# A gated layer on one core: product blocks summed by a strided reduction, the G projection moved, routing as a sign

## The chip, the cores and the metric

The kernel runs on one core of a Trainium2 chip. The metric is the device time of one execution in microseconds; lower is better. The engines named below are TensorE (PE, with its weight loads as PEld), VectorE (DVE), ScalarE (ACT), GpSimd (POOL) and SyncE (SP), each with its own in-order queue.

## The reference

Input x is 16 x 256 x 512 (16 blocks, 256 rows, 512 time steps), and a context of the same shape. The layer has two parts:

```
# part 1: per head of 8 rows, 32 heads
kv  = outer product of the context's rows            # i, j, head, l
y   = causal convolution of kv with ssm_kernel[head] + kv * D[head]
x   = x + tanh(g_xattn) * sum_i y[i, j] * q[i]       # q = layernorm(x)
# part 2: on each row of 512, 16 blocks of a sequence
z   = layernorm(x)
y   = silu(z_prev * w0 + z * w1)
q, k, v, g = silu(y Wq), y Wk, y Wv, y Wg            # then rotary on q and k
route = argmax over 2 of (v . router_w)              # one of two slots per head and position
q_exp, k_exp = q or k placed in the slot of its route, zero in the other; q scaled by score / count
o   = (q_exp k_exp^T masked causally) v              # then normalized per head
x   = x + tanh(g_ffn) * (silu(g) * o) Wout
```

A product of q_exp and k_exp is the plain product where both positions have the same route, and zero where they differ.

## The kernel before

The kernel works through 32 heads of part 1 (8 rows of 16 blocks: one 128 x 512 tile), and `step(h)` is a software pipeline written out in Python for h = -2 to 32. Each engine has its own order of work within a step, written by hand, with semaphores between them. A step h does the following for different tiles: `pre` prepares head h+2 (context products on POOL, normalized q), `front` does the convolution of head h+1, `back` the projections, routing and scores of tile h, `tail` the attention output and the output projection of the tile before.

TensorE's order in a step is: transposes of z (L361), convolution chunks 0 and 1 (L290), attention output (L337), convolution chunk 2, transposes of oT (L377), the last half block (L303, L306), q and k projections with the logits (L319), convolution chunk 3, the rank matmul (L402), transposes of qn, the V projection into bank 4 (L411), transposes of `gated` (L418), the transposes of the sums (L422, by `add_transposed`, L277), the G projection into bank 5 (L426), transposes of `qke` (L428, L431), the output projection (L440) and the scores (L352).

The convolution's result is multiplied with q on DVE (`multiply`, L743 and L747, and `multiply_last`), which leaves eight product blocks of 128 columns per chunk of 128 time steps in `z_terms`, four chunks in all. DVE adds the upper four blocks to the lower four (`add_halves`, L756: chunks 0 and 1 in one instruction, chunks 2 and 3 in one each). TensorE then sums the remaining four in PSUM while it transposes them: sixteen accumulating 128 x 128 transposes into bank 2, after which `xo_ps` is signalled. DVE reads bank 2 in L889 (x2), takes statistics (L892 to L900), POOL takes the root (L649), ACT makes the scaled mean and z (L610, L614), and z is transposed at the head of the next step.

Routing: the logit difference sits in bank 6. DVE writes `sel`, two 0/1 masks for q and k (L840, L841), and `u`, which is +0.5 or -0.5 (L842), used by the rank matmul that counts positions of a route. POOL applies the rotary factors to q and k (L667; L672 twice, one half of the columns each; L675, the sum into `rot_a`), and DVE expands the result into `qke` (L765, 1024 columns: two slots, each masked).

Three waits matter around the change. The V projection writes bank 4 and waits for `o_normed`, which DVE's L856 signals when it has read the attention output of the tile before from that bank. The transposes of `qke` wait for `qke_ready` (L765); those of k also for `gatedT_ready` (L877), which frees bank 7. The scores wait for `x2_ready`.

DVE's order after the half block is: L840 to L842, the add of chunks 0 and 1, L856, L861 (`gated`), the reciprocal L864, products of chunk 3, the adds of chunks 2 and 3, L873, L877, L765, L889 and the statistics, L903, L913 (output), then the four score masks (L760).

Of the kernel before, what the change touches and what calls it, by code (L numbers as in the profile page):

```python
# [13 lines left out]
P = 128  # L14
# [15 lines left out]
def flamingo_gated_layer(nc, x, ctx_t, g_xattn, g_ffn, ssm_kernel, ssm_D, conv_w, Wq, Wk, Wv, Wg,  # L30
# [35 lines left out]
    with ExitStack() as stack:  # L66
# [50 lines left out]
        u = sb("u", RH)  # L117
        sel = sb("sel", 2, RH, RATIO)
# [10 lines left out]
        setup = ExitStack()  # L129
        w_all = setup_sb("w_all", CH, PROJ)  # L130
# [4 lines left out]
        taps = setup_sb("taps", P + L)  # L135
        taps_p = setup.enter_context(nc.sbuf_tensor("taps_p", [P, 2, P + L], F32R))
        setup.close()

        y_raw = sb("y_raw", CH, P)
        qk_sb = sb("qk_sb", 2 * RH, HDK)  # L140
# [4 lines left out]
        qke = sb("qke", 2 * RH, RATIO * HDK)  # L145
# [7 lines left out]
        yT_p = parts("yT", CH, P)  # L153
# [111 lines left out]
        def _(eng):  # L265
# [5 lines left out]
            def add_transposed(h1):  # L271


                for c in range(CH):
                    eng.wait_ge(sum_done[max(c, 1)], h1 + 1)
                    for i in range(NROT):
                        ins = nc.tensor.matmul(bank[2][:, c * P:(c + 1) * P], z_terms[:, c, i * ROW:(i + 1) * ROW], ident,  # L277
                                               is_transpose=True, start=(c == 0 and i == 0), stop=(i == NROT - 1),
                                               skip_group_check=True)
                ins.then_inc(xo_ps, 1)  # L280
# [45 lines left out]
            def step(t, p, q, tail, back, front, pre):  # L326
# [72 lines left out]
                if back:  # L399
                    eng.wait_ge(u_ready, h + 1)  # L400
                    eng.wait_ge(qk_copied, h + 1)
                    nc.tensor.matmul(bank[6][:, 0:RH], rank, u[:, :], start=True, stop=True).then_inc(cnt_ps, 1)  # L402
# [16 lines left out]
                if front:  # L419
                    if pre:  # L420
                        eng.wait_ge(qx_ready, h + 3)
                    add_transposed(h + 1)  # L422
                if back:
                    if can_wait(h):
                        eng.wait_ge(mask_done[2], h)
                    project(bank[5], yT_p, w_all_p, G0, DV, g_ps, y_low, h + 1)  # L426
                    eng.wait_ge(qke_ready, h + 1)
                    transpose4(bank[3], lambda c: qke[:, 4 * c:4 * c + 4, :], qeT_ps)  # L428
                    if tail:
                        eng.wait_ge(gatedT_ready, h)  # L430
                    transpose4(bank[7], lambda c: qke[:, RH + 4 * c:RH + 4 * c + 4, :], keT_ps)  # L431
# [15 lines left out]
        def _(eng):  # L447
# [41 lines left out]
            def step(t, p, q, tail, back, front, pre):  # L489
# [60 lines left out]
                if back:  # L550
                    eng.wait_ge(q_ps, h + 1)
                    if can_wait(h):
                        eng.wait_ge(rot_prod, 3 * h)
                    eng.activation(qk_sb[:, 0:RH, :], bank[3][:, 0:DK].rearrange("p (a n) -> p a n", n=HDK),
                                   ACT.Silu)
                    eng.wait_ge(logit_ps, h + 1)
                    eng.activation(qk_sb[:, RH:2 * RH, :], bank[6][:, 0:DK].rearrange("p (a n) -> p a n", n=HDK),  # L557
                                   ACT.Copy).then_inc(qk_copied, 1)
                    if can_wait(h):
                        eng.wait_ge(rth1_ready, h)  # L560
                    eng.activation(ad[:, :], bank[6][:, DK:DK + RH], ACT.Abs).then_inc(ad_ready, 1)
                    eng.wait_ge(ad_ready, h + 1)
                    eng.activation(th[:, :], ad[:, :], ACT.Tanh, scale=0.5).then_inc(th_ready, 1)
                    eng.wait_ge(th_ready, h + 1)
                    eng.activation(th1[:, :], th[:, :], ACT.Copy, bias=1.0).then_inc(th1_ready, 1)
# [24 lines left out]
                if pre:  # L590
                    kv_round(p, 2, h + 2)
                    kv_round(p, 3, h + 2)
                if back:
# [3 lines left out]
                    eng.activation(gate_sb[:, :], bank[5][:, :], ACT.Silu).then_inc(gate_ready, 1)  # L597
                if back:
                    eng.wait_ge(qeT_ps, h + 1)
                    if can_wait(h):  # L600
                        for r in range(CH):
# [5 lines left out]
                                   ).then_inc(keT_sb, 1)  # L607
                if front:
# [11 lines left out]
        def _(eng):  # L620
# [30 lines left out]
            def step(t, p, q, tail, back, front, pre):  # L651
# [10 lines left out]
                if back:  # L662

                    eng.wait_ge(qk_copied, h + 1)
                    if can_wait(h):
                        eng.wait_ge(qke_ready, h)
# [3 lines left out]
                    for a in range(2):  # L670
                        s = const[:, C_SIN + a * hf:C_SIN + a * hf + 1]
                        eng.tensor_tensor(rot_b[:, :, a * hf:(a + 1) * hf], qk_sb[:, :, (1 - a) * hf:(2 - a) * hf],  # L672
                                          view(s, [[0, 2 * RH], [1, hf]]), ALU.mult).then_inc(rot_prod, 1)
                    eng.wait_ge(rot_prod, 3 * h + 3)
                    eng.tensor_tensor(rot_a[:, :, :], rot_a[:, :, :], rot_b[:, :, :], ALU.add).then_inc(rot_ready, 1)  # L675
# [12 lines left out]
        def _(eng):  # L688
# [3 lines left out]
            eng.memset(u[:, :], 0.0).then_inc(taps_ready, 1)  # L692
# [40 lines left out]
            def multiply(p, lc, h1):  # L733
# [3 lines left out]
                if lc == 0:  # L737
                    eng.wait_ge(qx_ready, h1 + 1)
                    if can_wait(h1):
                        eng.wait_ge(xo_ps, h1)  # L740
# [10 lines left out]
            def add_halves(chunks, h1):  # L751

                eng.wait_ge(mul_last, h1 + 1)
                eng.wait_ge(mul_done[chunks.stop - 1], h1 + 1)
                half = NROT * ROW
                eng.tensor_tensor(z_terms[:, chunks, 0:half], z_terms[:, chunks, 0:half], z_terms[:, chunks, half:2 * half],  # L756
                                  ALU.add).then_inc(sum_done[chunks.stop - 1], 1)
# [5 lines left out]
            def expand():  # L763

                eng.tensor_tensor(view(qke[:, 0, 0:1], [[RATIO * HDK, 2 * RH], [HDK, RATIO], [1, HDK]]),  # L765
                                  view(rot_a[:, 0, 0:1], [[HDK, 2 * RH], [0, RATIO], [1, HDK]]),
                                  view(sel[:, 0, 0, 0:1], [[RATIO, 2 * RH], [1, RATIO], [0, HDK]]),
                                  ALU.mult).then_inc(qke_ready, 1)
# [16 lines left out]
            def step(t, p, q, tail, back, front, pre):  # L785
# [47 lines left out]
                if back:  # L833
# [5 lines left out]
                    d = view(bank[6][:, DK:DK + 1], [[0, 2], [1, RH]])  # L839
                    eng.tensor_scalar(sel[:, :, :, 0], d, 0.0, None, ALU.is_le)  # L840
                    eng.tensor_scalar(sel[:, :, :, 1], d, 0.0, None, ALU.is_gt)  # L841
                    eng.tensor_scalar(u[:, :], bank[6][:, DK:DK + RH], 0.0, 0.5, ALU.is_gt, ALU.subtract).then_inc(u_ready, 1)  # L842
# [7 lines left out]
                if front:  # L850
                    add_halves(slice(0, 2), h + 1)
# [13 lines left out]
                if front:  # L865
                    multiply(p, 3, h + 1)
                    add_halves(slice(2, 3), h + 1)
                    add_halves(slice(3, 4), h + 1)
# [10 lines left out]
                if back:  # L879
                    eng.wait_ge(rot_ready, h + 1)  # L880
                    if can_wait(h):
                        eng.wait_ge(keT_ps, h)
                        eng.wait_ge(qeT_ps, h)
                    expand()
# [40 lines left out]
def shape_constants(NB, HDK):  # L925
# [8 lines left out]
    parts = [np.eye(P), same * HDK ** -0.5, rank, cos, cos, -sin, sin]  # L934
# [35 lines left out]
```

## Time and profile before

| | us |
|---|---|
| median of 3 runs | 923.17 (922.25 to 925.02) |
| profiled execution | 923.74 |
| its span | 921.9 |
| PE busy | 856.9 (93%) |
| DVE busy | 720.5 (78%) |
| ACT busy | 435.7 (47%) |
| POOL busy | 730.2 (79%) |

The span is the time from the first to the last record of the execution; what lies around it (1.8 us) is launch and end. Busy shares are averages over the whole span. Matmuls are pipelined, and the durations of neighbouring ones overlap: what one costs is read from the chain of waits, where each item begins when the one before it ends. In the order of time, "idle before" stands in brackets with the instruction that ended it.

### The profile page before, as it was taken

To read this page: it belongs to the slowest core of one execution; us is meant where nothing else is said; L and a number is where in the kernel's file an instruction comes from. 1 tells how busy PE (TensorE), PEld (TensorE's weight loads), DVE (VectorE), ACT (ScalarE), POOL (GpSimd) and SP (SyncE) were. 2 spreads that over 40 slices of the span, in tenths; PEclk is the share of its full clock that TensorE was granted. 3 is DMA by queue.
4 is the path that set the end of the run, shared out by engine and by line. 5 is a ranking of instruction groups with operands and counts; after the bars stand their busy time and mean duration, and the time that the engine had idled before them with its cause. 6 is when DMAs were issued, how large, how long until landed. Compare 5 with 4: busy or idle time off the path is not lost.

```text
span 921.9 us, 17871 instructions
## 1 busy us (share of the span) xinstructions
PE 856.9 (93%) x6528; PEld 724.3 (79%) x6528; DVE 720.5 (78%) x1528; ACT 435.7 (47%) x938; POOL 730.2 (79%) x613
## 2 busy tenths in 40 slices
PE   0578999999999999999999999999999999999973
PEld 0467888888888888888888888888888888888852
DVE  4867787987778889877787897778878877788742
ACT  2454544545545444554544545545445455454330
POOL 6568898788889888888899888888988888887331
PEclk9889999999999999999999999999999999999996
DMA  8211211222221122222211222222112222210000
GB/s 284 60 53 52 59 26 44 64 63 65 64 64 43 25 61 64 64 64 65 62 34 35 61 64 64 65 63 61 26 42 64 64 64 63 64 46 12 2 12 23
DMA packets 25990, 52.44 MB, mean 57 GB/s; under 512 B 2544, under 2 KB 3696, under 8 KB 25904
## 3 DMA queue, kind: packets, MB, share of 16 engines
q1 hardware_dynamic: 22304, 46.59, 18.7%
q10 hardware_dynamic: 3600, 4.72, 1.6%
q8 instruction: 52, 0.85, 0.4%
q14 instruction: 34, 0.28, 0.1%
HBM read 42.75 MB, written 8.55 MB: 56 GB/s over the span
## 4 chain that ended last, share of the span: by engine, by line
PE 86%; DVE 5%; issue 4%; DMA 1%; ACT 1%; POOL 1%; POOLq 0%; ACTq 0%; DVEq 0%
PE bank L319 37%; PE bank L290 23%; PE bank L268 9%; PE bank L277 6%; PE bank L352 4%; PE bank L337 4%; PE bank L303 2%; DMA w_all<-in_L_ffn_Wv 1%; PE bank L306 1%; DVE z_terms L756 1%; DVE w_all L719 0%; PE bank L402 0%; DVE z_terms L743 0%; DVE w_all_low L725 0%; POOLq L66 0%
## 5 line engine op out<-in xcount | busy, mean ns | idle before, releaser
L290 PE MATMUL bank<-kv_pair,toep 128*128 128x512 f32 x960 | 247.9, 405 | 11.4 <-DVE z_terms L747 6.6
L643 POOL TENSOR_TENSOR kv_pair<-kv,kv_pair 128x576 fp32r<-128x576 f32 x128 | 182.3, 1436 | 54.9 <-ACT kv_pair L487 54.9
L290 PEld LDWEIGHTS bank<-kv_pair,toep 128*128 128x128 f32 x960 | 177.2, 192 | 53.1 <-DVE z_terms L747 12.6
L634 POOL TENSOR_TENSOR kv<-kx 128x512 f32<-128x512 f32 x128 | 174.4, 1363 | 6.7 <-DMA const<-shape_consts 6.7
L649 POOL TENSOR_TENSOR o_rstd<-o_ve,minus_half 128x16 f32<-128x16 f32 x32 | 93.1, 2909 | 82.6 <-DVE o_ve L815 82.6
L487 ACT ACTIVATE kv_pair<-kv 128x576 fp32r<-128x576 f32 x128 | 87.9, 688 | 108.2 <-POOL kv L637 108.2
L319 PE MATMUL bank<-w_all_high,yT_high 128*128 128x512 f32 (+2 forms) x512 | 120.2, 356 | 2.8 <-DVE gated L856 2.8
L756 DVE TENSOR_TENSOR z_terms<-z_terms 128x512 f32<-128x512 f32 (+1 forms) x96 | 117.4, 1249 | 0.0
L319 PE MATMUL bank<-w_all_low,yT_high 128*128 128x512 f32 (+2 forms) x512 | 111.8, 340 | 0.0
L319 PE MATMUL bank<-w_all_high,yT_low 128*128 128x512 f32 (+2 forms) x512 | 106.1, 339 | 0.0
L913 DVE TENSOR_TENSOR out_sb<-bank,x 128x512 f32<-128x512 f32 x32 | 22.1, 691 | 105.6 <-PE bank L319 105.6
L760 DVE TENSOR_TENSOR att<-bank,const 128x512 f32<-128x512 f32 x128 | 79.5, 683 | 16.7 <-PE bank L352 16.7
L319 PEld LDWEIGHTS bank<-w_all_low,yT_high 128*128 128x128 f32 x512 | 83.7, 189 | 11.2
L319 PEld LDWEIGHTS bank<-w_all_high,yT_low 128*128 128x128 f32 x512 | 81.2, 188 | 11.5
L743 DVE TENSOR_TENSOR z_terms<-bank,qx 128x512 f32<-128x512 f32 x128 | 85.4, 667 | 4.3 <-PE bank L290 4.3
L319 PEld LDWEIGHTS bank<-w_all_high,yT_high 128*128 128x128 f32 x512 | 78.9, 190 | 8.9 <-DVE gated L856 3.2
L637 POOL TENSOR_TENSOR kv<-kx 128x64 f32<-128x64 f32 x128 | 73.5, 574 | 0.0
L747 DVE TENSOR_TENSOR z_terms<-bank,qx 128x384 f32<-128x384 f32 x128 | 69.9, 546 | 0.0
L667 POOL TENSOR_TENSOR rot_a<-qk_sb,const 128x512 f32<-128x512 f32 x32 | 66.2, 2069 | 2.5 <-ACT qk_sb L557 2.5
L277 PE MATMUL bank<-const,z_terms 128*128 128x128 f32 x512 | 62.5, 274 | 5.4 <-DVE z_terms L756 5.4
L503 ACT ACTIVATE y_raw<-bank,w_conv 128x128 f32<-128x128 f32 x128 | 36.6, 369 | 61.9 <-PE bank L268 61.9
L649 POOL TENSOR_TENSOR rstd<-ve,minus_half 128x1 f32<-128x1 f32 x64 | 41.2, 643 | 28.3 <-DVE ve L900 22.2
(102 smaller groups left out, 1588.7 us busy)
## 6 DMA issues: line engine op xcount, KB each, us to landing
toep<-taps_dram SPq DMA_DIRECT2D x32, 512.0 KB, 7.1
kx<-in_ctx SPq DMA_DIRECT2D x32, 384.0 KB, 7.4
x_in<-in_x SPq DMA_DIRECT2D x32, 256.0 KB
out_x<-out_sb SPq DMA_DIRECT2D x32, 256.0 KB
w_all<-in_L_ffn_Wv ACTq DMA_DIRECT2D x1, 1024.0 KB, 11.9
w_all<-in_L_ffn_Wg ACTq DMA_DIRECT2D x1, 1024.0 KB, 9.9
w_out<-in_L_ffn_Wout ACTq DMA_DIRECT2D x1, 1024.0 KB, 16.2
router<-in_L_ffn_router_w ACTq DMA_DIRECT2D x1, 512.0 KB, 7.3
```

The source lines that it names most:

```text
L268: ins = nc.tensor.transpose(dst[:, c * P:(c + 1) * P], src(c), ident)
L277: ins = nc.tensor.matmul(bank[2][:, c * P:(c + 1) * P], z_terms[:, c, i * ROW:(i + 1) * ROW], ident, is_transpose=True, start=(c == 0 and ...
L290: ins = nc.tensor.matmul(bank[lc % 2][:, :], toep[:, 1 - p, a, (lc - mc) * P:(lc - mc + 1) * P], kv_p[b][:, 1 - p, mc, 0:FULL], start=(mc ...
L319: ins = nc.tensor.matmul(dst[:, 0:cols], src_p[a][:, c, :], w_p[b][:, c, c0:c0 + cols], start=(i == 0 and c == 0), stop=(i == len(PASSES) ...
L487: eng.activation(kv_p[0][:, p, c, :], kv[:, c % 2, :], ACT.Copy).then_inc(kv_high[c], 1)
L634: eng.tensor_tensor(view(kv[:, c % 2, 0:FULL], [[ROW, NROT], [1, ROW]]), view(kx[:, p, c, 0:ROW], [[0, NROT], [1, ROW]]), view(kx[:, p, c, ...
L637: eng.tensor_tensor(kv[:, c % 2, FULL:FULL + HALF], kx[:, p, c, 0:HALF], kx[:, p, c, HALF:2 * HALF], ALU.mult).then_inc(kv_made[c], 1)
L643: eng.tensor_tensor(kv_p[1][:, p, c, :], kv[:, c % 2, :], kv_p[0][:, p, c, :].bitcast(F32), ALU.subtract).then_inc(kv_ready[c], 1)
L649: eng.tensor_tensor(dst[:, 0:n], src[:, 0:n], minus_half[:, 0:n], ALU.pow).then_inc(done, 1)
L743: eng.tensor_tensor(view(z_terms[:, lc, 0:1], [[ROW, NROT], [1, ROW]]), view(y[:, 0:1], [[ROW, NROT], [1, ROW]]), view(q, [[NB, NROT], [1, ...
L756: eng.tensor_tensor(z_terms[:, chunks, 0:half], z_terms[:, chunks, 0:half], z_terms[:, chunks, half:2 * half], ALU.add).then_inc(sum_done[ ...
L760: eng.tensor_tensor(att[:, r, :, :], bank[SCORE_BANKS[r]][:, :].rearrange("p (c n) -> p c n", c=CH), view(mask[:, 0:1], [[0, CH], [1, P]]) ...
```

## The change

Three things change together. First, the eight product blocks of a chunk are summed by one `tensor_reduce` on DVE that reads with a stride of 128 columns between the eight numbers of a sum and writes 128 sums to `z_sum` (the memory of `y_raw`); TensorE transposes the four chunks once each. Second, the order changes: on TensorE the G projection comes before the sums' transposes; on ACT the gate follows `gatedT` directly, and the two late `kv_round` calls are spread; on DVE the last step of `qke` comes before L873 and L877. Third, routing: `qke` holds q or k in its even columns (written by POOL's rotary sum) and the same times a sign of +1 or -1 in its odd columns (written by DVE); the causal factor is halved in the constants, so that equal signs give the product and different ones zero. `sel` is gone, `u` has a copy for k, and the two half-width products of POOL are one instruction. Memory is laid out anew so that `y_raw` and `yT` don't lie over weights still in use at the start.

```diff
-        sel = sb("sel", 2, RH, RATIO)
+        u = sb("u", 2, RH)
+        z_sum = y_raw
-        qke = sb("qke", 2 * RH, RATIO * HDK)
+        qke = sb("qke", 2 * RH, HDK, RATIO)
...
-            def add_transposed(h1):
+            def transpose_sums(h1):
                 for c in range(CH):
-                    eng.wait_ge(sum_done[max(c, 1)], h1 + 1)
-                    for i in range(NROT):
-                        ins = nc.tensor.matmul(bank[2][:, c * P:(c + 1) * P], z_terms[:, c, i * ROW:(i + 1) * ROW], ident,
-                                               is_transpose=True, start=(c == 0 and i == 0), stop=(i == NROT - 1),
-                                               skip_group_check=True)
+                    eng.wait_ge(sum_done[c], h1 + 1)
+                    ins = nc.tensor.transpose(bank[2][:, c * P:(c + 1) * P], z_sum[:, c, :], ident)
                 ins.then_inc(xo_ps, 1)
...
+                if back:
+                    if can_wait(h):
+                        eng.wait_ge(mask_done[2], h)
+                    project(bank[5], yT_p, w_all_p, G0, DV, g_ps, y_low, h + 1)
                 if front:
                     if pre:
                         eng.wait_ge(qx_ready, h + 3)
-                    add_transposed(h + 1)
-                if back:
-                    if can_wait(h):
-                        eng.wait_ge(mask_done[2], h)
-                    project(bank[5], yT_p, w_all_p, G0, DV, g_ps, y_low, h + 1)
+                    transpose_sums(h + 1)
...
-                if pre:
-                    kv_round(p, 2, h + 2)
-                    kv_round(p, 3, h + 2)
                 if back:
                     ... gate_sb (Silu) ...
+                if pre:
+                    kv_round(p, 2, h + 2)
                 if back:
                     ... qeT, keT ...
+                if pre:
+                    kv_round(p, 3, h + 2)
...
-                    for a in range(2):
-                        s = const[:, C_SIN + a * hf:C_SIN + a * hf + 1]
-                        eng.tensor_tensor(rot_b[:, :, a * hf:(a + 1) * hf], qk_sb[:, :, (1 - a) * hf:(2 - a) * hf],
-                                          view(s, [[0, 2 * RH], [1, hf]]), ALU.mult).then_inc(rot_prod, 1)
-                    eng.wait_ge(rot_prod, 3 * h + 3)
-                    eng.tensor_tensor(rot_a[:, :, :], rot_a[:, :, :], rot_b[:, :, :], ALU.add).then_inc(rot_ready, 1)
+                    sin = const[:, C_SIN:C_SIN + 1]
+                    eng.tensor_tensor(view(rot_b[:, 0, 0:1], [[HDK, 2 * RH], [hf, 2], [1, hf]]),
+                                      view(qk_sb[:, 0, hf:hf + 1], [[HDK, 2 * RH], [-hf, 2], [1, hf]]),
+                                      view(sin, [[0, 2 * RH], [hf, 2], [1, hf]]), ALU.mult).then_inc(rot_prod, 1)
+                    eng.wait_ge(rot_prod, 2 * h + 2)
+                    if can_wait(h):
+                        eng.wait_ge(keT_ps, h)
+                        eng.wait_ge(qeT_ps, h)
+                    eng.tensor_tensor(qke[:, :, :, 0], rot_a[:, :, :], rot_b[:, :, :], ALU.add).then_inc(rot_ready, 1)
...
-            def add_halves(chunks, h1):
-                eng.wait_ge(mul_last, h1 + 1)
-                eng.wait_ge(mul_done[chunks.stop - 1], h1 + 1)
-                half = NROT * ROW
-                eng.tensor_tensor(z_terms[:, chunks, 0:half], z_terms[:, chunks, 0:half], z_terms[:, chunks, half:2 * half],
-                                  ALU.add).then_inc(sum_done[chunks.stop - 1], 1)
+            def sum_terms(c, h1):
+                eng.wait_ge(mul_last, h1 + 1)
+                eng.wait_ge(mul_done[c], h1 + 1)
+                if can_wait(h1):
+                    eng.wait_ge(xo_ps, h1)
+                eng.tensor_reduce(z_sum[:, c, :], view(z_terms[:, c, 0:1], [[1, ROW], [ROW, 2 * NROT]]), AX_X, ALU.add
+                                  ).then_inc(sum_done[c], 1)
...
-            def expand():
-                eng.tensor_tensor(view(qke[:, 0, 0:1], [[RATIO * HDK, 2 * RH], [HDK, RATIO], [1, HDK]]),
-                                  view(rot_a[:, 0, 0:1], [[HDK, 2 * RH], [0, RATIO], [1, HDK]]),
-                                  view(sel[:, 0, 0, 0:1], [[RATIO, 2 * RH], [1, RATIO], [0, HDK]]),
-                                  ALU.mult).then_inc(qke_ready, 1)
+            def signed_copy():
+                eng.scalar_tensor_tensor(out=qke[:, :, :, 1], in0=qke[:, :, :, 0], scalar=2.0,
+                                         in1=view(u[:, 0, 0:1], [[1, 2 * RH], [0, HDK]]), op0=ALU.mult, op1=ALU.mult
+                                         ).then_inc(qke_ready, 1)
...
-                    d = view(bank[6][:, DK:DK + 1], [[0, 2], [1, RH]])
-                    eng.tensor_scalar(sel[:, :, :, 0], d, 0.0, None, ALU.is_le)
-                    eng.tensor_scalar(sel[:, :, :, 1], d, 0.0, None, ALU.is_gt)
-                    eng.tensor_scalar(u[:, :], bank[6][:, DK:DK + RH], 0.0, 0.5, ALU.is_gt, ALU.subtract).then_inc(u_ready, 1)
+                    eng.tensor_scalar(u[:, :, :], view(bank[6][:, DK:DK + 1], [[0, 2], [1, RH]]), 0.0, 0.5, ALU.is_gt, ALU.subtract).then_inc(u_ready, 1)
...
-                    add_halves(slice(0, 2), h + 1)
+                    sum_terms(0, h + 1)
+                    sum_terms(1, h + 1)
...
-                    add_halves(slice(2, 3), h + 1)
-                    add_halves(slice(3, 4), h + 1)
+                    sum_terms(2, h + 1)
+                    sum_terms(3, h + 1)
+                if back:
+                    eng.wait_ge(rot_ready, h + 1)
+                    if can_wait(h):
+                        eng.wait_ge(keT_ps, h)
+                        eng.wait_ge(qeT_ps, h)
+                    signed_copy()
...
-    parts = [np.eye(P), same * HDK ** -0.5, rank, cos, cos, -sin, sin]
+    parts = [np.eye(P), same * HDK ** -0.5 / 2, rank, cos, cos, -sin, sin]
```

In the new order `multiply` of chunk 0 waits for the last sum and no longer for `xo_ps`.

## Rows read from the trace of the kernel before

**Rows 1.** Stretches, busy us (x count) of PE, PEld, DVE, ACT, POOL, then clock

```profile
356.00:412.00 56.00, 55.82 (x428) 47.50 (x427) 46.44 (x103) 28.29 (x65) 48.45 (x41) 1.00 0.20 53
```

**Rows 2.** Chain of waits, one step: start us, us, what

```profile
413.43 2.78 PE bank L319 x12
416.21 0.44 PE bank L268 x4
416.65 1.75 PE bank L277 x16
418.40 2.78 PE bank L319 x12
...
422.05 2.75 PE bank L319 x12
424.80 1.10 PE bank L352 x32
...
439.86 2.78 PE bank L319 x12
```

**Rows 3.** Chain of waits, transposes of z of steps 1 and 30

```profile
81.05 0.59 PE bank L268 x4
...
849.21 0.59 PE bank L268 x4
```

**Rows 4.** Order of time, one step on DVE: start us, us, engine, line, operation

```profile
406.70 0.69 DVE L812 TENSOR_REDUCE o_var<-o_sq 128x16 f32<-128x512 f32 x1
...
410.77 0.18 DVE L840 TENSOR_SCALAR sel<-bank 128x32 f32<-128x32 f32 x1
...
411.05 1.22 DVE L756 TENSOR_TENSOR z_terms<-z_terms 128x1024 f32<-128x1024 f32 x1
...
412.18 0.69 DVE L856 TENSOR_TENSOR gated<-bank,o_rstd 128x512 f32<-128x512 f32 x1
...
413.16 0.76 PEld L319 LDWEIGHTS bank<-w_all_high,yT_high 128*128 128x128 f32 x4
...
415.06 2.43 DVE L756 TENSOR_TENSOR z_terms<-z_terms 128x512 f32<-128x512 f32 x2
...
418.09 1.56 DVE L765 TENSOR_TENSOR qke<-rot_a,sel 128x1024 f32<-128x1024 f32 x1
```

**Rows 5.** Order of time at the start, DVE and POOL

```profile
14.67 1.70 DVE L702 TENSOR_TENSOR router_d<-router 128x512 f32<-128x512 f32 x1 [0.66 <-DMA w_all<-in_L_ffn_Wv]
...
15.78 0.77 POOL L637 TENSOR_TENSOR kv<-kx 128x64 f32<-128x64 f32 x1
...
44.05 1.28 DVE L756 TENSOR_TENSOR z_terms<-z_terms 128x512 f32<-128x512 f32 x2
```

**Rows 6.** Order of time, then the chain, last step with a convolution

```profile
860.60 2.06 DVE L756 TENSOR_TENSOR z_terms<-z_terms 128x1024 f32<-128x1024 f32 x1
...
863.31 0.76 PEld L319 LDWEIGHTS bank<-w_all_high,yT_high 128*128 128x128 f32 x4 [0.73 <-DVE gated L856]
...
863.31 3.06 PE bank L319 x12
```

**Rows 7.** Order of time, POOL at step 0 and in the step of rows 4

```profile
64.11 1.27 POOL L667 TENSOR_TENSOR rot_a<-qk_sb,const 128x512 f32<-128x512 f32 x1 [2.53 <-ACT qk_sb L557]
...
411.23 2.18 POOL L667 TENSOR_TENSOR rot_a<-qk_sb,const 128x512 f32<-128x512 f32 x1
```

**Rows 8.** Order of time, from the sums to z in the same step

```profile
419.58 0.74 DVE L889 SCALAR_TENSOR_TENSOR x<-bank,gates,x_in 128x512 f32<-128x512 f32 x1
...
421.37 0.14 DVE L900 TENSOR_SCALAR ve<-mv 128x1 f32<-128x1 f32 x1
...
423.76 0.81 ACT L614 ACTIVATE z<-x,nmr,rstd 128x512 f32<-128x512 f32 x1
```

**Rows 9.** Order of time, TensorE at step 0

```profile
73.36 0.71 PEld L277 LDWEIGHTS bank<-const,z_terms 128*128 128x128 f32 x4 [1.20 <-DVE z_terms L756]
...
74.13 2.06 PE L319 MATMUL bank<-w_all_high,yT_high 128*128 128x512 f32 x4
```

More of the change, by code:

```diff
@@ L116, in flamingo_gated_layer @@
         ad = sb("ad", RH)
-        u = sb("u", RH)
-        sel = sb("sel", 2, RH, RATIO)
+        u = sb("u", 2, RH)
         th = sb("th", RH)
@@ L129, in flamingo_gated_layer @@
         setup = ExitStack()
+        taps = setup_sb("taps", P + L)
+        taps_p = setup.enter_context(nc.sbuf_tensor("taps_p", [P, 2, P + L], F32R))
         w_all = setup_sb("w_all", CH, PROJ)
@@ L134, in flamingo_gated_layer @@
         router_d = setup_sb("router_d", RH * HDV)
-        taps = setup_sb("taps", P + L)
-        taps_p = setup.enter_context(nc.sbuf_tensor("taps_p", [P, 2, P + L], F32R))
         setup.close()
         y_raw = sb("y_raw", CH, P)
+        z_sum = y_raw
+        yT_p = parts("yT", CH, P)
         qk_sb = sb("qk_sb", 2 * RH, HDK)
@@ L152, in flamingo_gated_layer @@
         out_sb = sb("out_sb", 2, L)
-        yT_p = parts("yT", CH, P)
         gatedT_p = parts("gatedT", CH, P)
@@ L401, in step @@
                     eng.wait_ge(qk_copied, h + 1)
-                    nc.tensor.matmul(bank[6][:, 0:RH], rank, u[:, :], start=True, stop=True).then_inc(cnt_ps, 1)
+                    nc.tensor.matmul(bank[6][:, 0:RH], rank, u[:, 0, :], start=True, stop=True).then_inc(cnt_ps, 1)
                 if pre:
@@ L418, in step @@
                     transpose4(bank[7], lambda c: gated[:, c * P:(c + 1) * P], gatedT_ps)
-                if front:
-                    if pre:
-                        eng.wait_ge(qx_ready, h + 3)
-                    add_transposed(h + 1)
                 if back:
@@ L426, in step @@
                     project(bank[5], yT_p, w_all_p, G0, DV, g_ps, y_low, h + 1)
+                if front:
+                    if pre:
+                        eng.wait_ge(qx_ready, h + 3)
+                    transpose_sums(h + 1)
+                if back:
                     eng.wait_ge(qke_ready, h + 1)
-                    transpose4(bank[3], lambda c: qke[:, 4 * c:4 * c + 4, :], qeT_ps)
+                    transpose4(bank[3], lambda c: qke[:, 4 * c:4 * c + 4, :, :], qeT_ps)
                     if tail:
                         eng.wait_ge(gatedT_ready, h)
-                    transpose4(bank[7], lambda c: qke[:, RH + 4 * c:RH + 4 * c + 4, :], keT_ps)
+                    transpose4(bank[7], lambda c: qke[:, RH + 4 * c:RH + 4 * c + 4, :, :], keT_ps)
                 if tail:
@@ L552, in step @@
                     if can_wait(h):
-                        eng.wait_ge(rot_prod, 3 * h)
+                        eng.wait_ge(rot_prod, 2 * h)
                     eng.activation(qk_sb[:, 0:RH, :], bank[3][:, 0:DK].rearrange("p (a n) -> p a n", n=HDK),
@@ L589, in step @@
                                    ).then_inc(gatedT_high, 1)
-                if pre:
-                    kv_round(p, 2, h + 2)
-                    kv_round(p, 3, h + 2)
                 if back:
@@ L607, in step @@
                                    ).then_inc(keT_sb, 1)
+                if pre:
+                    kv_round(p, 3, h + 2)
                 if front:
@@ L665, in step @@
                     if can_wait(h):
-                        eng.wait_ge(qke_ready, h)
+                        eng.wait_ge(rot_ready, h)
                     eng.tensor_tensor(rot_a[:, :, :], qk_sb[:, :, :], view(const[:, C_COS:C_COS + 1], [[0, 2 * RH], [1, HDK]]),
@@ L691, in _ @@
             eng.tensor_tensor(taps[0:NH, P:P + 1], taps[0:NH, P:P + 1], d_tap[0:NH, :], ALU.add).then_inc(taps_zero, 1)
-            eng.memset(u[:, :], 0.0).then_inc(taps_ready, 1)
+            eng.memset(u[:, :, :], 0.0).then_inc(taps_ready, 1)
             eng.wait_ge(taps_high, 1)
@@ L739, in multiply @@
                     if can_wait(h1):
-                        eng.wait_ge(xo_ps, h1)
+                        eng.wait_ge(sum_done[CH - 1], h1)
                 q = qx[:, 1 - p, lc, 0:1]
```

4 lines of the change are left out of this document (removed).

## The prediction

> **What bounds the kernel now.** I read the stretches first, then the chain of waits, then the order of time on each engine. In 356 to 412 us TensorE is busy for 55.82 of 56.00 us at full granted clock, DVE for 46.44, POOL for 48.45 [rows 1]. TensorE is thus the bound in the middle, and the others have room only on average. The chain of waits is almost nothing but TensorE there, one item after the other without a gap [rows 2]. One step (one head) is 26.43 us, read between two starts of the V projection, 413.43 and 439.86; between two starts of the transposes of z, 81.05 and 849.21, lie 29 steps of 26.49 [rows 2, 3]. So what TensorE no longer issues is won, unless another engine hands something over too late. The whole question is how late DVE is at each hand-over.
>
> **TensorE's own work.** The sixteen accumulating transposes of the product blocks are one item of the chain, 1.75 us, 109 ns each. Four plain transposes of the same size are 0.44 us (those of `gated`) [rows 2]. The change leaves four: 1.75 - 0.44 = 1.31 us less per step. The G projection (2.78) moves ahead of them and costs the same there [rows 2]. With no new wait a step would be 26.46 - 1.31 = 25.15 us.
>
> **DVE before the V projection: the step that decides.** TensorE may write bank 4 only when DVE has read it in L856 (`o_normed`). Now L856 runs from 412.18 to 412.87, and the first weight load of the V projection starts at 413.16: 0.29 us of slack [rows 4]. In front of L856 stands the sum of chunks 0 and 1. It is one add of 1024 results now, 1.22 us, with the next instruction 1.13 after its start [rows 4]. The change puts two reductions there, each reading 1024 numbers. The trace has no such reduction, so its price is bounded. L812 reads 512 contiguous numbers in 0.69 us; 512 more at one per cycle, the rate between the add of 1024 (1.13) and the adds of 512 when nobody disturbs them (two in 1.28, row at 44.05), are 0.53 [rows 4, 5]. That gives 1.22 us for one, 1.13 from start to start. Below, it can't be under an undisturbed add of 512 results, which reads the same 1024 numbers through two inputs: 0.61 [rows 5]. Above, the slowest strided read in the trace is the subtraction L702, 512 results in 1.70 us, or 3.4 us for 1024 [rows 5]. I take 1.13, because L812 is the same operation and only its stride differs. Two of them are 2.26, that is +1.13. Of the three small instructions L840 to L842 (410.77 to 411.05, 0.28 us) one of 32 columns is left, started 0.10 before its successor: -0.18 [rows 4]. L856 therefore ends 0.95 us later, at 413.82, and the weight load can start at 413.87 and not at 413.16: 0.71 us late. DVE's clock up to here hangs on the end of the scores (masks, then convolution products, then statistics), which is TensorE's own work, so the delay doesn't average out; it returns in each step.
>
> The trace has this stall once. In the last step with a convolution the add took 2.06 us instead of 1.22, and the V projection's weight load stood idle for 0.73 until L856 was done, 863.31 [rows 6]. The chain then gives the projection 3.06 us instead of 2.78, since the overlap of loads with the matmuls before is lost too. From 413.87 it ends at 416.93 against 416.21 now: TensorE loses 0.72 of the 1.31. Net 0.59 per step, a step of 25.87.
>
> **Between POOL and DVE.** Instructions with two inputs in SBUF exclude each other on these two engines: POOL's L667 took 2.18 us while the add ran beside it, and 1.27 at step 0 where nothing did [rows 7]. The reductions have one input; I take it that they neither wait nor block. POOL's rotation gets earlier by this and by the merged `rot_b`; it was never late for DVE. I take POOL's strided write to `qke` at nothing: it is no longer waited for until 419.1; if it cost another 0.5 us, it would hold L861 for as long and use up slack only.
>
> **After the V projection.** All times from here are of the old clock, shifted as above. V ends at 416.93, the transposes of `gated` at 417.37, G at 420.15, the sums' transposes at 420.59, those of `qke` at 421.46. On DVE 2.19 us lie now between L856's end and the adds of chunks 2 and 3 (L861, reciprocal, products of chunk 3) [rows 4]. I add 0.8, since L861 meets POOL's third rotary instruction, 413.8 to 415.1 by three times 1.27 from 411.23 [rows 7]. So the reductions start at 416.8 and take 2.26 (the two disturbed adds 2.43 [rows 4]); the last sum is there at 419.1, needed at 420.15. The signed copy has 512 results and two inputs: 0.7 us against L765's 1.56 [rows 4]; it ends at 419.8 and is needed at 420.59. L877 follows and ends at 420.5, needed at 421.03. All is in time, by 0.5 to 1.0 us. What the cover costs if it is gone: each microsecond beyond that is one of the step.
>
> **The loop through z.** The transposes of the sums will end 4.7 us before those of the next z (0.87, 2.75, 1.10) and not 7.5 us [rows 2]. The chain behind them: L889 at 419.58 to L900 done at 421.51 is 1.93; from there to z done at 424.57 it is 3.06 now, with three copies ahead in ACT's queue; without them I put 1.9, of which z is 0.81 [rows 8]. With 3.85 us it fits by 0.9; with the whole 3.06 it would be 0.3 late. DVE must be free at 420.6, and is by 0.1. `kv_round(3)`, moved between `keT` and the mean on ACT, has its product by then and ends before the root does. POOL runs its last two `kv_rest` about 1.7 us later against TensorE; its idle time, 7.55 of 56 us or 3.6 per step [rows 1], takes that up.
>
> **Start and end.** At step -1, where DVE is the bound, four reductions (4.5) stand for adds of 1.2 and 1.28 [rows 4, 5], less 0.7 of transposes: +1.3. At step 0 TensorE waited 1.20 us for the last sum with the G projection behind it, which then ran at the lower clock, 2.06 us for four matmuls [rows 9]. Now it runs in that wait: the z transposes come at 78.3 and not 81.05 [rows 3], -2.7. The last step with a convolution has a stall already; there 1.31 - 0.1 = 1.2 is won. Behind it nothing.
>
> **Sum.** 29 x 0.59 = 17.1, and 1.2, and 2.7 - 1.3 = 1.4: 19.7 us off. The profiled execution took 923.74 (span 921.9), so 904.0; it lies 0.6 above the median of the runs. I forecast 904.
>
> **A rule that speaks against it.** The only strided read on DVE, L702 (every second float), took 1.70 us, but POOL held an instruction until 15.78, and from there it took 0.6, as an undisturbed one: no cost of stride to be seen [rows 5]. The Trainium skill (Advanced Engine Details and Errata, SBUF Cachelines) says that SBUF has lines of 16 bytes and that an access to a new line each time pays a penalty; a stride of 8 bytes has two hits on a line, the new reads, 512 bytes apart, none. It gives no figure; by that rule the reductions are slower and the sum above falls. No row here shows it.
>
> **Rivals.**
> - A, strided reads at half rate (chance 0.12). A reduction then takes 2.2 us from start to start. L856 ends 2.14 later still, V ends at 419.07; the last sum comes at 422.8 against G's end at 422.3, and the copy and L877 hold the last transposes by another 0.7. A step is then 29.0: 923.7 + 30 x 2.6 = 1001. It decides from 1.42 us per reduction (0.3 above mine) on: there the 0.59 is gone. Against it: L702; for it: nothing in the profile has such a stride.
> - B, DVE's second half is the bound (0.15). The signed copy or L861 meets one more POOL instruction (1.2 us) and L877 and L889 come 1.2 later. The transposes of k wait 0.7 and z is 0.2 late: a step of 26.5, and 921. For it: the adds of chunks 2 and 3 took 1.2 us each where 0.61 is undisturbed [rows 4, 5]. Against: POOL has done its products at 418.2 and waits for rsqrt by then.
> - C, no stall (0.08): something ahead of L856 gets shorter, such as the reduction at its lower bound. 31 x 1.31 = 41 off: 883.
> - The forecast (0.65): 895 to 914, from reductions 0.15 shorter to 0.15 longer (30 x 0.3 = 9 us each way).
>
> **Range and chances.** 890 to 925 takes in the forecast and B and leaves out A and C, 0.20. This kernel's measurement tells 0.3%, 2.8 us. Faster: 0.65 + 0.08 + 0.04 of B = 0.77; same: 0.07; slower: 0.12 + 0.04 = 0.16.
>
> **What would show it.** Right: a step of 25.9 us; on TensorE one idle item of 0.7 us per step ahead of the V projection, released by L856; the sums' transposes at 0.44; reductions of 1.22 us; L667 back at 1.3 us. Wrong: reductions well off 1.22; waits of TensorE for `qke`, for the low part of `gated` or for z; or no idle time ahead of V.

## The result and the profile after

The changed kernel takes 988.73 us (median of 4 runs, 987.17 to 994.32) against 923.63 beside it: 1.072 times as long, 95% interval 1.067 to 1.076. The forecast was 904, in 890 to 925. The profiled execution has a span of 985.4 us against 921.9.

Two of the costliest groups of the changed kernel's page. Each line gives line, engine, operation, out<-in, shapes and count, then busy us and mean ns of one, then the engine's idle time before them and what ended it.

```profile
L759 DVE TENSOR_REDUCE y_raw<-z_terms 128x128 f32<-128x1024 f32 x128 | 246.3, 1963 | 0.1
L316 PE MATMUL bank<-w_all_high,yT_high 128*128 128x512 f32 (+2 forms) x512 | 121.5, 359 | 61.2 <-DVE gated L856 61.2
```

A reduction takes 1.96 us and not the 1.22 of the forecast, and TensorE stands idle for 61 us in all until L856 is done. The next rows are one step in the order of time, on DVE, POOL and TensorE's weight loads (start us, us). They are the counterpart of [rows 4] and [rows 7]:

```profile
435.68 0.69 DVE L814 TENSOR_REDUCE o_var<-o_sq 128x16 f32<-128x512 f32 x1
...
439.75 0.18 DVE L841 TENSOR_SCALAR u<-bank 128x32 f32<-128x32 f32 x1
439.87 3.87 DVE L759 TENSOR_REDUCE y_raw<-z_terms 128x128 f32<-128x1024 f32 x2
440.21 1.30 POOL L666 TENSOR_TENSOR rot_a<-qk_sb,const 128x512 f32<-128x512 f32 x1
...
443.67 0.67 DVE L856 TENSOR_TENSOR gated<-bank,o_rstd 128x512 f32<-128x512 f32 x1
...
444.39 0.76 PEld L316 LDWEIGHTS bank<-w_all_high,yT_high 128*128 128x128 f32 x4 [2.25 <-DVE gated L856]
```

The two reductions occupy DVE for 3.80 us (439.87 to 443.67), 1.90 each from start to start. The rest is as forecast. `u` starts 0.12 us before its successor, POOL's first rotary product (L667 before, now L666) is back at 1.30 us, and the V projection's weight load starts as soon as L856 is done (444.34). Only the price of the reductions is another. Later in a step two small waits follow, for the copy into `qke` and for L883 (L877 before):

```profile
422.51 0.68 DVE L768 SCALAR_TENSOR_TENSOR qke<-qke,u 128x512 f32<-128x512 f32 x1
...
423.24 0.42 PEld L268 LDWEIGHTS bank<-const,qke 128*128 128x128 f32 x4 [0.46 <-DVE qke L768]
...
423.92 0.42 PEld L268 LDWEIGHTS bank<-const,qke 128*128 128x128 f32 x4 [0.26 <-DVE gatedT_low L883]
```

**Where 63.5 us of span went.** The scores (L349, L352 before) of step 0 start at 84.28 (79.87 before): 4.4 us. The 30 steps from there to the scores of step 30, at 938.70 (874.89 before), take 854.4 us and not 795.0: 59.4. The tail is 0.3 shorter. Of the 30 steps most take 28.2 us, but ten take about 28.95 and the first 29.76. Two neighbouring stretches of one step's length differ in the granted clock, which is the number behind the busy us of PE, PEld, DVE, ACT and POOL:

```profile
300.00:328.20 28.20, 26.36 (x190) 22.01 (x191) 24.41 (x47) 13.21 (x29) 19.10 (x19) 0.94 0.19 53
328.20:356.40 28.20, 25.80 (x194) 21.06 (x193) 25.11 (x48) 13.54 (x29) 19.79 (x19) 1.00 0.19 52
```

In the first of them, the matmuls behind TensorE's idle 2 us run slower for a while. The second and third group below took 1.10 and 1.09 us in the G projection of the same step, and the granted clock is 0.50 in the stretch from 303 to 305 us:

```profile
301.76 1.20 PE L316 MATMUL bank<-w_all_high,yT_high 128*128 128x512 f32 x4 [2.01 <-DVE gated L856]
302.79 1.71 PE L316 MATMUL bank<-w_all_low,yT_high 128*128 128x512 f32 x4
304.30 1.91 PE L316 MATMUL bank<-w_all_high,yT_low 128*128 128x512 f32 x4
```

```profile
303.00:305.00 2.00, 2.00 (x6) 1.60 (x5) 2.00 (x5) 0.00 (x0) 1.88 (x3) 0.50 0.00 0
```

So the clock went from 2.4 to 1.2 GHz for a part of this projection after the idle time. It does so in about every third step. The eleven long steps take 10 x 0.75 + 1.5 = 9 us of the 59.

### The profile page after: what moved, and what is told of

It reads as the page before. It is cut to its first block and busy times, and to the rows that moved or that the text cites. A ratio compares the mean times of both kernels' runs of the same rounds, so it can differ in the third digit from the quotient of the medians.

```text
span 985.4 us, 17102 instructions
## 1 busy us (share of the span) xinstructions
PE 851.8 (86%) x6144; PEld 697.1 (71%) x6144; DVE 827.6 (84%) x1496; ACT 443.5 (45%) x938; POOL 641.4 (65%) x581
## 5 line engine op out<-in xcount | busy, mean ns | idle before, releaser
L759 DVE TENSOR_REDUCE y_raw<-z_terms 128x128 f32<-128x1024 f32 x128 | 246.3, 1963 | 0.1
L633 POOL TENSOR_TENSOR kv<-kx 128x512 f32<-128x512 f32 x128 | 159.9, 1249 | 6.5 <-DMA const<-shape_consts 6.5
L316 PE MATMUL bank<-w_all_low,yT_high 128*128 128x512 f32 (+2 forms) x512 | 119.5, 358 | 0.0
L316 PE MATMUL bank<-w_all_high,yT_low 128*128 128x512 f32 (+2 forms) x512 | 113.2, 355 | 0.0
L316 PEld LDWEIGHTS bank<-w_all_low,yT_high 128*128 128x128 f32 x512 | 88.2, 198 | 12.5
L316 PEld LDWEIGHTS bank<-w_all_high,yT_low 128*128 128x128 f32 x512 | 86.8, 199 | 13.5
L581 ACT ACTIVATE v_sb<-bank 128x512 f32<-128x512 f32 x32 | 19.1, 598 | 149.6 <-PE bank L316 149.6
L636 POOL TENSOR_TENSOR kv<-kx 128x64 f32<-128x64 f32 x128 | 55.6, 435 | 0.0
L592 ACT ACTIVATE gate_sb<-bank 128x512 f32<-128x512 f32 x32 | 19.1, 598 | 68.7 <-PE bank L316 68.7
```

Source lines behind the costliest of these rows:

```text
L316: ins = nc.tensor.matmul(dst[:, 0:cols], src_p[a][:, c, :], w_p[b][:, c, c0:c0 + cols], start=(i == 0 and c == 0), stop=(i == len(PASSES) ...
L633: eng.tensor_tensor(view(kv[:, c % 2, 0:FULL], [[ROW, NROT], [1, ROW]]), view(kx[:, p, c, 0:ROW], [[0, NROT], [1, ROW]]), view(kx[:, p, c, ...
L636: eng.tensor_tensor(kv[:, c % 2, FULL:FULL + HALF], kx[:, p, c, 0:HALF], kx[:, p, c, HALF:2 * HALF], ALU.mult).then_inc(kv_made[c], 1)
L759: eng.tensor_reduce(z_sum[:, c, :], view(z_terms[:, c, 0:1], [[1, ROW], [ROW, 2 * NROT]]), AX_X, ALU.add).then_inc(sum_done[c], 1)
```

## The experiments

All times are medians beside runs of the kernel before on the same chip, and a ratio is the time over that of the kernel before, with its 95% interval. Diffs are cut short and are against the changed kernel, if nothing else is said. A step is read between two starts of the scores.

### Distance or number of results

```diff
-  view(z_terms[:, c, 0:1], [[1, ROW], [ROW, 2 * NROT]])      # 128 results of 8, 512 bytes apart
+  view(z_terms[:, c, 0:1], [[2 * NROT, ROW], [1, 2 * NROT]]) # e1_contiguous: neighbours
+  view(z_terms[:, c, 0:1], [[1, ROW], [ROW, NROT]])          # e2_four_blocks: half the numbers
```

> The changed kernel, but each reduction reads its 1024 numbers in the order of memory (8 neighbours per result) and not 512 bytes apart; the number of results, 128, stays, so the sums are of the wrong blocks and only the time is of use. The changed kernel has 1.96 us per reduction. Theory S (the distance between the numbers costs): 1.22 us per reduction, an idle 0.7 us ahead of the V projection, 895 to 914 us in all. Theory R (each result costs, 128 here against the 16 of L814): 1.96 us and 988 us, as changed.

> The changed kernel, but each reduction sums blocks 0 to 3 alone and leaves out 4 to 7: 512 numbers, the same distance, the same 128 results. Theory S: (1.96 - 0.15) / 1024 = 1.77 ns per number read, so 0.15 + 512 x 1.77 ns = 1.06 us per reduction, and 893 to 903 us. Theory R: 0.15 + 0.53 for the numbers + 128 x 5.8 ns for the results = 1.43 us, and 912 to 925 us.

e1_contiguous: 905.93 us, 0.980 of before (0.979 to 0.982). Below are the group of its reductions, from the groups by form, and the start of the V projection, from the order of time:

```profile
L759 DVE TENSOR_REDUCE y_raw<-z_terms 128x128 f32<-128x1024 f32 x128 | 149.7, 1210 | 0.1
```

```profile
405.15 0.68 DVE L856 TENSOR_TENSOR gated<-bank,o_rstd 128x512 f32<-128x512 f32 x1
...
405.89 0.76 PEld L316 LDWEIGHTS bank<-w_all_high,yT_high 128*128 128x128 f32 x4 [0.74 <-DVE gated L856]
```

A reduction takes 1.21 us, TensorE's weight loads are idle for 0.74 us ahead of V, and a step takes 25.89 (scores at 364.39 and 390.28). This is the forecast kernel, in its price, its wait (0.71), its step (25.87) and its time (904).

e2_four_blocks: 898.06 us, 1.074 us per reduction. Theory S said 0.15 + 512 x 1.77 ns = 1.06; the 1.43 of theory R is refuted. So the distance between the numbers costs, (1963 - 1210) / 1024 = 0.74 ns per number on top of about 1.04, and the number of results doesn't.

### From which distance on

```diff
+  view(z_terms[:, c, 0:1], [[6, ROW], [(2, 4, 8, 16)[c], 2 * NROT]])   # 8, 16, 32, 64 bytes
```

> The changed kernel with a different distance between the eight numbers of a result in each chunk's reduction: 8 bytes in chunk 0, 16 in chunk 1, 32 in chunk 2, 64 in chunk 3, 24 bytes from result to result; the sums are of the wrong numbers and only the durations are of use. If the price comes with every number that does not follow its neighbour, all four take 1.96 us. If it comes with a new 16-byte line per number, chunk 0 takes less (towards 1.2 to 1.6) and chunks 1 to 3 the same 1.96. If it grows with distance, the four rise one after the other.

The run took 948.65 us (one execution, for its durations alone). The rows are DVE's order of time: chunks 0 and 1 together, then chunks 1, 2 and 3, each by itself in a narrower stretch:

```profile
423.26 3.15 DVE L759 TENSOR_REDUCE y_raw<-z_terms 128x128 f32<-128x1024 f32 x2
```

```profile
424.39 2.01 DVE L759 TENSOR_REDUCE y_raw<-z_terms 128x128 f32<-128x1024 f32 x1
```

```profile
429.14 2.14 DVE L759 TENSOR_REDUCE y_raw<-z_terms 128x128 f32<-128x1024 f32 x1
```

```profile
431.18 1.97 DVE L759 TENSOR_REDUCE y_raw<-z_terms 128x128 f32<-128x1024 f32 x1
```

Chunk 0, 8 bytes apart, takes 424.39 - 423.26 = 1.13 us from start to start, as contiguous ones do. At 16, 32 and 64 bytes a reduction takes 2.01, 2.14 and 1.97 us, and 1.96 at 512 bytes. The jump lies between 8 and 16 bytes, and the price doesn't grow with the distance behind it.

The Trainium skill (Advanced Engine Details and Errata, SBUF Cachelines) says of lines of 16 bytes that it takes at least two hits on one to absorb the access. These four durations agree, and e1_contiguous has given the figure, 0.74 ns per number. L702, which reads every second float, had two hits.

### The rest of the change by itself

```diff
+  # e3_old_sums: add_halves and the sixteen accumulating transposes of before, in the new order
```

> The changed kernel with its new order and its routing by a sign, but with the sums of before: adds of halves on DVE and sixteen accumulating transposes. If the reductions alone made the change slow, TensorE is the bound again with a step of 26.4 us, and the start gains up to 3 us: 918 to 924. If the new order or the routing has a cost of its own, TensorE shows new waits for qke, z or gatedT and the time is over 928.

920.14 us, 0.995 (0.994 to 0.997). From 300 to 600 us TensorE waits for DVE only ahead of the convolution (L289, 0.2 us per step, as L290 did before), and the scores follow each other by 26.4 us (366.98, 393.40). The new order and the routing by a sign have no cost of their own and gain 4 us, nearly all at the start (the scores of step 0 begin at 75.48 instead of 79.87). The signed copy took 1.63 us there, against 0.68 in the changed kernel, while POOL had products of its own, and no wait for it shows.

```diff
+  # e11_sums_alone: the kernel before with the reductions and four plain transposes, old order, old routing
```

> The kernel before with the strided reductions and the four plain transposes alone: its old order and its old routing (and the new memory layout, which the sums need). The reductions are then late twice: V waits 2.4 us for L856, and the transposes of the sums, still ahead of the G projection, wait another 2.8 us with G behind them. A step of 30 us, 1020 to 1040. If only the wait ahead of V costs, 990.

1054.62 us, 1.141 (1.138 to 1.143): 66 us more than the changed kernel, and 15 more than the upper end of what I expected. Waits of TensorE in 300 to 600 us (total, times, longest):

```profile
PEld bank L277 <- DVE y_raw L754: 27.1, 20, 1.7
PEld bank L316 <- DVE gated L855: 23.6, 10, 2.4
```

Both waits of the expectation are there, 2.36 and 2.7 us per step. Steps are 30.2 us, and from the sixth on every third is 31.6 to 31.8. The expectation had left out the clock; these eight steps take about 11 us more than the others. The wait of 2.7 us is about as long as the G projection (2.78), which stands in that place in the changed kernel and has no such wait there. That G ahead of the sums is what spares the changed kernel this wait is argued from these two lengths; the routing differs as well, and no run moves G by itself.

### The reductions behind L856

```diff
-                    sum_terms(0, h + 1); sum_terms(1, h + 1)      # ahead of L856
+                    sum_terms(0, h + 1); sum_terms(1, h + 1)      # e4_sums_late: behind the reciprocal
```

> The changed kernel with the reductions of chunks 0 and 1 behind L856, L861 and the reciprocal on DVE. If the wait of the V projection is all that costs, it goes (2.2 us per step) and the time is about 915. If DVE is the bound for the rest of the step as well, which four reductions of 1.9 us make likely, the wait moves to the transposes of the sums and of qke: a step of 27.9 us, 970 to 978.

999.15 us, 1.081 (1.079 to 1.083), slower than the changed kernel. No wait ahead of the V projection is left. The largest waits of TensorE in 300 to 600 us (total, times, longest) are

```profile
PEld bank L276 <- DVE y_raw L759: 25.3, 22, 1.7
...
PEld bank L268 <- DVE qke L768: 4.6, 10, 0.5
```

The wait has only moved: four reductions make DVE the bound of the whole step. Its step is 28.15 us, near the expected 27.9. But every second or third lasts 29.7, such as the one from 372.58 to 402.31 at a granted clock of 0.94. The expectation of 970 to 978 had left that out: 14 steps longer by 1.6 make 22 us.

### The distance on the writing side

```diff
+  view(z_terms[:, lc, 0:1], [[1, NROT], [2 * NROT, ROW]])    # e8_interleaved: products written 32 bytes apart
+  view(z_terms[:, c, 0:1], [[2 * NROT, ROW], [1, 2 * NROT]]) # and read as neighbours
```

> The distance on the writing side: the products are written 32 bytes apart, eight blocks interleaved, and the reduction reads them contiguously in 1.21 us; the second product's rotation is left out, so that the numbers are not the reference's, but count and size of the instructions are. If DVE's writes pay nothing for distance: 905 us as with the contiguous reduction. If they pay as the reads did, 0.75 ns per number, L745 goes from 0.67 to 1.05 and L749 from 0.55 to 0.83, and 3 us more per step stand on DVE: over 950.

In this run the rotation of the second product is left out too, so that its sums are not the reference's; the count and the size of the instructions are. 1012.15 us, 1.093 (1.091 to 1.095). From the groups by form:

```profile
L745 DVE TENSOR_TENSOR z_terms<-bank,qx 128x512 f32<-128x512 f32 x128 | 145.0, 1133 | 4.1 <-PE bank L287 4.1
L749 DVE TENSOR_TENSOR z_terms<-bank,qx 128x384 f32<-128x384 f32 x128 | 115.8, 905 | 0.0
```

They were 667 and 546 ns in the changed kernel: (1133 - 667) / 512 = 0.91 ns per number written 32 bytes apart, a little more than a read pays. The reductions are back at 1.20 us, and still TensorE waits 2.3 us per step for L856, with the slower products ahead of it. Moving the distance to the other side gains nothing.

### Adds instead of reductions

```diff
+  # e5_tree_two: contiguous adds, 8 blocks to 4 (two instructions), 4 to 2 (one), eight transposes
+  # e6_tree_three: and 2 to 1 (one), four transposes
```

> The changed kernel, its order and its routing, but the sums on DVE are adds of contiguous halves, two levels deep: eight blocks to four (chunks 0 and 1 in one instruction ahead of L856, chunks 2 and 3 in one), then four to two (all chunks in one, 1024 results); TensorE sums the last two in eight accumulating transposes. If contiguous reads and little work ahead of L856 are what the change lacked: L856 in time, no wait of the V projection, 26.46 - 8 x 0.109 = 25.6 us per step, about 895. If DVE's second half is then the bound (adds have two inputs and meet POOL, 1.2 us each), waits for qke and gatedT_low of up to 1 us: 905 to 925.

> As the one before with a third level (two blocks to one, 512 results, all chunks) and four plain transposes. TensorE alone would need 25.15 us per step: about 882. DVE has 2.9 us of adds behind the products of chunk 3 instead of 2.3 with the reductions forecast; if POOL holds each of the three for another 0.5 us, the transposes of the sums and of qke wait for about 1 us and the time is 900 to 912.

e5_tree_two: 916.16 us, 0.990 (0.987 to 0.993), in the second of the expected ranges. L856 is in time. But behind the products of chunk 3 the two adds take 2.35 and 2.07 us beside POOL's products, and TensorE waits about 0.4 us per step for the last (L769). The step is 26.1 and not 25.6.

e6_tree_three: 975.53 us, 1.053 (1.050 to 1.056), far from what I expected. One of its steps, DVE and then POOL in the order of time:

```profile
409.74 2.35 DVE L759 TENSOR_TENSOR z_terms<-z_terms 128x1024 f32<-128x1024 f32 x1
412.19 2.07 DVE L767 TENSOR_TENSOR z_terms<-z_terms 128x1024 f32<-128x1024 f32 x1
414.29 0.69 DVE L772 TENSOR_TENSOR y_raw<-z_terms 128x512 f32<-128x512 f32 x1
414.91 1.70 DVE L781 SCALAR_TENSOR_TENSOR qke<-qke,u 128x512 f32<-128x512 f32 x1
```

```profile
410.97 2.21 POOL L634 TENSOR_TENSOR kv<-kx 128x512 f32<-128x512 f32 x1
413.14 1.30 POOL L637 TENSOR_TENSOR kv<-kx 128x64 f32<-128x64 f32 x1
```

The adds and the signed copy have two inputs in SBUF, as POOL's products have. While both engines had such an instruction, each took longer: 2.35, 2.07 and 1.70 us on DVE against 1.2, 1.2 and 0.7 at their shortest in the run, 2.21 and 1.30 on POOL against 1.2 and 0.3. The sequence lasts 6.9 us where I had 2.9 plus the copy. TensorE waits for its end twice in each step (300 to 600 us: total, times, longest):

```profile
PE bank L277 <- DVE y_raw L772: 11.9, 11, 1.1
PE bank L269 <- DVE qke L781: 10.0, 11, 0.9
```

Steps of 27.7 and, with a clock of 0.96 over the run, some of 29.3 follow. The reductions, with one input, were not held like this in any run: 1.20 to 1.22 us in e1_contiguous and 1.85 to 2.04 in the changed kernel, beside POOL's products or not.

### Two neighbours of one line

Product blocks i and i+4 are interleaved in pairs. The products are then written 8 bytes apart, and a reduction reads two neighbours, jumps 1024 bytes and reads the next two.

```diff
-  view(z_terms[:, lc, 0:1], [[ROW, NROT], [1, ROW]])              # first products
+  view(z_terms[:, lc, 0:1], [[2 * ROW, NROT], [2, ROW]])
-  first = 4 * ROW + NB;  view(..., [[ROW + NB, NROT - 1], [1, ROW]])  # second
+  first = 2 * NB + 1;    view(..., [[2 * (ROW + NB), NROT - 1], [2, ROW]])
-  eng.tensor_reduce(z_sum[:, c, :], view(z_terms[:, c, 0:1], [[1, ROW], [ROW, 2 * NROT]]), AX_X, ALU.add)
+  eng.tensor_reduce(z_sum[:, c, :], view(z_terms[:, c, 0:1], [[2, ROW], [2 * ROW, NROT], [1, 2]]), AX_XY, ALU.add)
+  # (the products of the last half block likewise)
```

> The changed kernel with product blocks i and i+4 interleaved in pairs, so that the products are written 8 bytes apart and each reduction reads neighbours two by two (two numbers of each 16-byte line, then 1024 bytes on); it computes the reference. If a read is free as long as two numbers come from one 16-byte line: 1.21 us per reduction. If DVE's writes are free at 8 bytes as well: L745 stays 0.68 us and the time is that of the contiguous reduction, 903 to 909. If the writes pay at 8 bytes as they did at 32: L745 1.13 us, about 1010. If the jump of 1024 bytes between pairs costs half of the full price: 1.6 us per reduction, 945 to 955.

> As the one before, with the reduction of chunk 1 moved behind L856, L861 and the reciprocal, so that one reduction (1.13 us from start to start) stands ahead of L856 where one add of 1.13 stood in the kernel before. If the wait of the V projection is what was left to gain, it goes and a step is 25.2 to 25.4 us: 885 to 892. If the second half then holds TensorE (the last sum, qke or the low part of gated up to 0.5 us late): 893 to 905. No gain over the one before would say that DVE bounds the whole step.

e9_pairs: 906.38 us, 0.980 (0.978 to 0.982). Its reductions take 1.21 us and its products stay at 0.68 and 0.55. So writing 8 bytes apart costs nothing, and neither does the jump of 1024 bytes between pairs that are read. What is left is the forecast wait ahead of V.

e10_pairs_one_late moves the reduction of chunk 1 behind L856 and takes the wait away: 885.47 us, 0.958 (0.956 to 0.960), faster than both kernels. One step, DVE and the weight loads in the order of time:

```profile
419.63 1.22 DVE L760 TENSOR_REDUCE y_raw<-z_terms 128x128 f32<-128x1024 f32 x1
420.77 0.68 DVE L856 TENSOR_TENSOR gated<-bank,o_rstd 128x512 f32<-128x512 f32 x1
421.48 1.59 DVE L861 TENSOR_TENSOR gated<-gated,gate_sb 128x512 f32<-128x512 f32 x1
421.85 0.77 PEld L317 LDWEIGHTS bank<-w_all_high,yT_high 128*128 128x128 f32 x4
...
423.16 1.15 DVE L760 TENSOR_REDUCE y_raw<-z_terms 128x128 f32<-128x1024 f32 x1
```

L856 is done at 420.77 + 0.68 = 421.45, and the load starts at 421.85 without a wait. TensorE's only wait for DVE behind V is 0.2 us per step for L884 (L883 in the changed kernel). The step is 25.25 us in the median (one of them, 331.32 to 356.54, 25.22), and 25.15 was the estimate of what TensorE's own work alone would need.

## Why the prediction was wrong

The step that failed is the price of a reduction, in the part on DVE before the V projection: 1.13 us from start to start, "because L812 is the same operation and only its stride differs". The stride was the price: 1.90 us. L812 differs in the number of results too (16 and not 128), but that costs nothing: e1_contiguous, with 128 results and the stride alone taken back, has 1.21 us and the forecast time. The upper bound by L702 (3.4 us) held the price, but L702 was read as evidence that a stride is free when it reads 8 bytes apart, which e7_distances shows to be the last free distance of those tried. The rule on lines of 16 bytes, of the Trainium skill (Advanced Engine Details and Errata, SBUF Cachelines), stood in the text, with the remark that the new reads have no second hit. Rival A, slow strided reads, got a chance of 0.12.

The other terms, one by one:

- TensorE's saving (1.31 us per step, G moved at no cost): right. With no wait ahead of V, in e10_pairs_one_late, the step is 25.25 us, 1.2 below the 26.45 of before.
- The wait for L856 as what decides, and its size for a given price: right. With 1.21 us it is 0.74 (0.71 forecast), with 1.96 it is 2.25 (0.71 + 2 x 0.77 = 2.25).
- Reductions neither wait for POOL nor hold it: right within 0.2 us (L666 at 1.30; reductions from 1.85 to 2.04 us in the changed kernel).
- Signed copy 0.7, POOL's strided write at nothing: right in the changed kernel (0.68; the rotary sum took 1.27 us). Where the copy met POOL's products it took longer, up to 1.04 in e1_contiguous and 1.63 on average in e3_old_sums, without a wait of TensorE.
- After V all in time: right for e1_contiguous. With the true price the second half is late, as rival A said: a wait of 0.46 for `qke` and one of 0.26 for L883. The loop through z fits, as forecast: no wait for z shows from 300 to 600 us.
- The start, -1.4: wrong by the same price. Step 0 is 4.4 us later. Ahead of its scores TensorE waited 1.95 and 1.46 us for the last sums and then ran at the lower clock. In e1_contiguous the scores of step 0 begin at 78.07, 1.8 us earlier than before.
- Rival A was the mechanism. It gave 1001 us for 2.2 us per reduction, with a step of 29.0. With 1.90 the step is 28.2, and 0.3 more on average by the long steps, whose lower clock no part of the prediction had. It named 1.42 us as the point from which the gain is gone, and 1.90 is well beyond it.
- Rival B, DVE's second half as the bound through POOL, did not decide anything in the changed kernel. It is what happened to e6_tree_three, where the signed copy took 1.70 us.

Left open is why the clock falls in only every third step at the same idle time; the 9 us are read from the long steps of one trace. Other traces show where it didn't fall. In e7_distances TensorE was idle for 1.3 us ahead of V in every step, no step was long (27.0 to 27.2 from the second on) and the granted clock was 1.00 from 100 to 900 us. In e6_tree_three it was idle for 2.0 us per step in two pieces, and seven of the steps behind the first were long. No run tests the clock by itself.

## What to carry to other kernels

When a change trades contiguous instructions for one strided instruction, price the stride first, by a row with the same number of hits per 16 bytes. A row with a smaller stride says nothing of it: here 8 bytes were free and 16 bytes cost the full price. If the layout can be paired, so that the reduction reads two neighbours at a time and the products are written 8 bytes apart, the reduction costs no more than a contiguous one (1.21 us in e9_pairs). When an engine's sum of work still fits, look at what stands ahead of the instruction that another engine waits for, and move only as much behind it as the rest of the step can carry: one reduction of 1.13 us could go there, two of 1.90 could not.

## What the runs showed of the hardware

- A `tensor_reduce` on DVE reads 1024 fp32 numbers per partition from SBUF in 1.96 to 2.14 us when they lie 16, 32, 64 or 512 bytes apart (e7_distances, the changed kernel). It takes 1.21 when they are neighbours or come in pairs (e1_contiguous, e9_pairs), and 1.13 from start to start at 8 bytes, as contiguous ones do.
- DVE's products, written as fp32 to SBUF, cost 0.91 ns more per number at 32 bytes apart (e8_interleaved) and nothing more at 8 bytes (0.68 us for 512 in e9_pairs).
- With TensorE idle for 2 us per step ahead of V, in the changed kernel, the granted clock was 0.94 over a long step, about every third, and 1.00 over the next (300 to 356 us). With 1.3 us in e7_distances and 0.5 us in e1_contiguous (0.74 of its weight loads) no such steps came.
- Instructions with two inputs in SBUF on DVE and on POOL lengthened each other when they met (2.35 us against 1.2 for an add, e6_tree_three). A reduction with one input changed by less than 0.2 us.
